# The routed experts of a Hyena block: results kept in SBUF, four chunks of 64 groups

## The reference

```python
grouped = x.reshape(B, g, t, d)                     # 256 groups of t = 32 tokens, d = 512
logits = jnp.einsum('bgtd,des->bgtes', grouped, controller) + tie
perm = (logits == jnp.max(logits, axis=-3, keepdims=True)).astype(x.dtype)
dispatched = jnp.einsum('bgtd,bgtes->bgesd', grouped, perm)
inner = jax.nn.relu(jnp.einsum('bgesd,desf->bgesf', dispatched, f1) + bias)
intermediate = jnp.einsum('bgesf,esfd->bgesd', inner, f2)
out = jnp.einsum('bgesd,bgtes->bgtd', intermediate, perm)
x = _layernorm(x + out)
```

## Time and profile before

| | |
|---|---|
| Runs | 2234.15, 2235.25, 2236.55 us; median 2235.25 us |
| Span of the profiled execution | 2229.5 us (its own time around the span isn't listed; the median of the runs is 5.75 us above it) |
| Mean granted clock of TensorE | 0.916 |
| Busy | PE 1895.0 us, DVE 1405.8, ACT 933.4, POOL 513.0 |
| Moved | 513.73 MB, mean 230 GB/s |

### The profile page before, as it was taken

How to read it: one execution, slowest core, us unless ns; L and a number is a source line. 1 busy time by engine, 2 the same in 40 slices (tenths; PEclk the granted TensorE clock), 3 DMA queues, 4 the chain that set the end, 5 groups by cost and what they waited for, 6 DMA issues and landing times. The chain is left out here.

```text
span 2229.5 us, 34871 instructions
## 1 busy us (share of the span) xinstructions
PE 1895.0 (85%) x12342; PEld 1285.3 (58%) x12342; DVE 1405.8 (63%) x2748; ACT 933.4 (42%) x1755; POOL 513.0 (23%) x410
## 2 busy tenths in 40 slices
PE   7999999999999699999969999996757676576444
PEld 6777777777777443444458888885636352352000
DVE  5877777877778454555558889885434354354344
ACT  4444444444444344444445555552323232242222
POOL 0100010001000044454455555551302020020000
PEclk9999999999999899999999999998889797697555
DMA  5134233333333577888767777773997999999999
GB/s 167 67 116 140 100 114 114 126 116 114 107 114 113 175 202 226 221 243 229 208 196 248 246 245 237 237 243 136 356 392 286 383 336 413 405 326 413 373 391 344
DMA packets 287298, 513.73 MB, mean 230 GB/s; under 512 B 26480, under 2 KB 105366, under 8 KB 278806
## 3 DMA queue, kind: packets, MB, share of 16 engines
q1 hardware_dynamic: 277909, 494.71, 65.8%
q10 hardware_dynamic: 9216, 16.78, 2.0%
HBM read 309.78 MB, written 201.62 MB: 229 GB/s over the span
## 5 line engine op out<-in xcount | busy, mean ns | idle before, releaser
L90 PE MATMUL p_pu<-p_xT_high,p_win_high 128*128 128x512 f32 (+1 forms) x816 | 329.9, 404 | 14.2 <-DVE p_win_low L85 12.0
L91 PE MATMUL p_pu<-p_xT_high,p_win_low 128*128 128x512 f32 (+1 forms) x816 | 313.3, 384 | 0.0
L92 PE MATMUL p_pu<-p_xT_low,p_win_high 128*128 128x512 f32 (+1 forms) x816 | 313.1, 384 | 0.0
L447 ACT ACTIVATE p_t<-p_pu,p_tbias,p_taps 128x512 f32<-128x512 f32 (+1 forms) x192 | 146.5, 763 | 358.2 <-PE p_pu L92 357.3
L85 POOL TENSOR_TENSOR p_xT_low<-p_xT,p_xT_high 128x2048 fp32r<-128x2048 f32 (+1 forms) x16 | 71.3, 4456 | 618.0 <-ACT p_xT_high L80 618.0
L564 DVE SCALAR_TENSOR_TENSOR p_t<-p_pu,p_taps,p_t 128x256 f32<-128x256 f32 (+1 forms) x384 | 208.6, 543 | 6.8
L849 POOL TENSOR_TENSOR q_y<-q_y 128x512 f32<-128x512 f32 x128 | 160.2, 1270 | 194.8 <-DVE q_y L870 194.8
L90 PEld LDWEIGHTS p_pu<-p_xT_high,p_win_high 128*128 128x128 f32 x816 | 155.4, 190 | 46.8 <-DVE p_xT_low L85 10.2
L92 PEld LDWEIGHTS p_pu<-p_xT_low,p_win_high 128*128 128x128 f32 x816 | 154.9, 190 | 32.8
L91 PEld LDWEIGHTS p_pu<-p_xT_high,p_win_low 128*128 128x128 f32 x816 | 155.4, 190 | 25.4
L870 DVE TENSOR_TENSOR q_y<-q_pg,q_v 128x512 f32<-128x512 f32 x256 | 158.0, 674 | 2.1 <-PE q_pg L779 1.8
(11 more groups left out here) (144 smaller groups left out, 3773.7 us busy)
## 6 DMA issues: line engine op xcount, KB each, us to landing
s_I<-e_out SPq DMA_DIRECT2D x64, 1024.0 KB, 8.5
q_av<-s_SV SPq DMA_DIRECT2D x64, 512.0 KB, 4.3
s_Z<-q_z SPq DMA_DIRECT2D x128, 256.0 KB, 3.2
o_zin<-s_Z SPq DMA_DIRECT2D x64, 512.0 KB, 3.9
k_shared<-s_I SPq DMA_DIRECT2D x32, 1024.0 KB, 11.9
e_taken<-s_I SPq DMA_DIRECT2D x32, 1024.0 KB, 11.5
e_out<-s_X SPq DMA_DIRECT2D x48, 512.0 KB, 8.6
s_X<-p_t SPq DMA_DIRECT2D x64, 256.0 KB, 2.3
```

What stands on the lines that cost most here:

```text
L90: pe.matmul(out, a[0], b[0], start=start, stop=False)
L91: pe.matmul(out, a[1], b[0], start=False, stop=False)
L92: return pe.matmul(out, a[0], b[1], start=False, stop=stop)
L447: nc.scalar.activation(t[r][m % 2][:, c], pu[(W + n) % 3][:, c], ACT.Identity, bias=tbias[:, w:w + 1], scale=taps[:, w, 2:3]).then_inc(t_o ...
```

## The change

The experts phase is written anew, and the choices' turning at the end of `output_phase` goes.

- *Chunks.* Four chunks of 64 groups (`GC`), each with all 128 experts. The rows tile `taken` has the layout (d block, pair of groups, expert, group of the pair); a pair of groups is interleaved element by element. It keeps its size, 32768 floats per partition.
- *Choices.* K stays resident. Per half chunk PE turns eight blocks of it (`choices`), ACT copies them to `picked`, and POOL spreads them (`pick`). TOOK and TAKE are gone.
- *Dispatch.* 8 matmuls of 256 moving columns per tile; 16 tiles per chunk. The token rows are read once.
- *Layers.* 32 quads per chunk. `layer1` has 64 moving columns, read from `rows` as 32 pairs of 8 bytes, 1 KB apart. `hidden` writes the pair of experts of each 64 rows side by side, with zeros (or what the bias makes of them, cancelled by `back`) where rows and columns don't belong together, as one scalar_tensor_tensor. `layer2` has the second weights as stationary operand (64 rows x 128 columns) and the hidden values as the moving one (128 columns), so the result comes out with d on the partitions, and one copy puts it over the quad's dispatched rows in `rows`. Scratch I is gone. The weights are loaded once per chunk, four times in all.
- *Turn.* Before the combine of a tile, PE turns its results back, 16 blocks of 128 x 128 per tile, reading every second element of `rows` as stationary operand; ACT and DVE copy them to one of three tiles `it`.
- *Combine.* As before, with K as stationary operand and `it` as moving. Turns and combines of a chunk are interleaved with the dispatch of the next, one tile of each per step; those of the last chunk stand alone.
- *PSUM.* Choices, dispatch, layer 2 and turns share a ring of three pairs of banks (`pun`); every unit has a number and a taker, ACT or DVE. Layer 1 and combine share two more banks, cleared by `clear` once per chunk.

```diff
-    pt = [ps(f"pt{s}", [P, 4, ES]) for s in range(2)] + pc
...
-            for v in range(2 * UNITS):
-                turn_take(v)
...
-            for u in range(UNITS):
-                store_unit(u)
...
+    GC = 64
+    CHUNKS = G // GC
+    TC = GC * GT // P
+    GP = GC // 2
+    NU, NF, NX, NI, NP, NR, NL, NX0 = 3, 4, 2, 3, 2, 3, 8, 8
...
+        rows = taken[:].rearrange("p (k b e g) -> p k b e g", k=DT, b=GP, e=ES)
...
+        def numbered():
+            for c in range(CHUNKS + 1):
+                if c < CHUNKS:
+                    yield "pick", c, 0, ON_ACT
+                for m in range(TC + 1):
+                    if c and m < TC:
+                        yield "turn", c - 1, 2 * m, ON_ACT
+                        yield "turn", c - 1, 2 * m + 1, ON_DVE if c < CHUNKS or m % 2 else ON_ACT
+                    if c < CHUNKS and m:
+                        yield "send", c, 2 * m - 2, ON_ACT
+                        if m == TC // 2 - 1:
+                            yield "pick", c, 1, ON_ACT
+                        yield "send", c, 2 * m - 1, ON_ACT if c and m % 2 else ON_DVE
+                if c < CHUNKS:
+                    for i in range(Q):
+                        yield "quad", c, i, (ON_ACT, ON_DVE)[i % 2]
...
             def load_weights(n):
-                s = n % NF
                 if n >= NF:
-                    sp.wait_ge(o_ps, ONE + n - NF + 1)
-                sp.dma_start(ff[s], A["ffn_f"][:, n % Q]).then_inc(ff_in[s], 16)
+                    b = n - NF
+                    sp.wait_ge(u_ps, ONE + number["quad", b // Q, b % Q] + 1)
+                sp.dma_start(ff[n % NF][:], A["ffn_f"][:, n % Q]).then_inc(ff_in[n % NF], 16)
...
+                if m >= LATE:
+                    x = (m - LATE) % NL
...
+                    if m >= NR:
+                        sp.wait_ge(res_st[m % NR], ONE + m // NR * 16)
+                    sp.dma_start(res_of(m), xr[m]).then_inc(res_in[m % NR], 16)
...
+            def bank_pair(u):
+                if u >= NU:
+                    pe.wait_ge(taken_ok[taker[u - NU]], ONE + taken_by[u - NU])
+                return pun[u % NU]
...
+            def choices(c, b):
...
+                    x = pe.transpose(to[:, m, :], K[:, t:t + P], ident[:])
...
+                        w = pe.matmul(to[:, h, a * 2 * ES:(a + 1) * 2 * ES], x[r, k * P:(k + 1) * P],
+                                      pick[j % NP][r].rearrange("p e g -> p (e g)"), start=True, stop=True)
...
-                        m = pe.matmul(ph[s][r, :], ff[w][:, 0, k * P + e * EF:k * P + (e + 1) * EF],
-                                      rows[:, k, 4 * i + e, :], start=(k == 0), stop=(k == DT - 1))
+                        x = pe.matmul(to[r, :, e % 2, :], ff[w][:, 0, k * P + e * EF:k * P + (e + 1) * EF],
+                                      rows[:, k, :, 4 * i + e, :], start=(k == 0), stop=(k == DT - 1))
...
-                    m = pe.matmul(po[e // 2][:, e % 2, :], hid[s][r, :], ff[w][r, 1, :],
-                                  start=True, stop=True)
+                        x = pe.matmul(to[:, h, k * P:(k + 1) * P], ff[w][r, 1, k * P:(k + 1) * P], hid[s][r, :],
+                                      start=True, stop=True)
...
+            def turn(c, n):
+                to = bank_pair(number["turn", c, n])
+                for g in range(2):
+                    for k in range(DT):
+                        x = pe.transpose(to[:, g, k * P:(k + 1) * P], rows[:, k, n, :, g], ident[:])
+                x.then_inc(u_ps, 1)
...
+                    x = pe.matmul(pq[j % 2][r, :], K[:, j * P + g * GT:j * P + (g + 1) * GT], it[n % NI][:, g % 2, :],
+                                  start=True, stop=True)
...
+                for m in range(TC + 1):
+                    if c and m < TC:
+                        turn(c - 1, 2 * m)
+                        turn(c - 1, 2 * m + 1)
+                    if c < CHUNKS and m:
+                        dispatch(c, 2 * m - 2)
+                        if m == TC // 2 - 1:
+                            choices(c, 1)
+                        dispatch(c, 2 * m - 1)
+                    if c and c < CHUNKS and m < TC:
+                        combine(c - 1, m)
+                    if c == CHUNKS and m:
+                        combine(c - 1, m - 1)
...
+                dve.scalar_tensor_tensor(hid[n % 2][:].rearrange("p (b x) -> p b x", x=4), ph[n % 2].rearrange("p (b x) -> p b x", x=4),
+                                         nbias[:, i:i + 1], back[:, i:i + 1, :].to_broadcast([P, GP, 4]), ALU.max, ALU.add
+                                         ).then_inc(hid_ok, 1)
```

More of the change, by code:

```diff
@@ L884, in output_phase @@
     UNITS = N1 // UG
[L885 removed]
+    NZ, NR = 3, 6
     with ExitStack() as ctx:
@@ L1122, in _ @@
                     finish(n - 1)
-            for u in range(UNITS):
-                keep_took(act, nc.scalar.copy, 2 * u)
         @block.vector
@@ L1517, in _ @@
[L1517 to L1534 removed]
+            pe.wait_ge(consts, ONE + 48)
@@ L1568, in _, with take @@
-            for m in range(NT0, NT):
-                close(m)
-            finish(NT - 1)
+                act.dma_start(dst[m], res_of(m)).then_inc(stored_to(m), 16)
+            def take(kind, c, n):
+                keep(act, nc.scalar.copy, ON_ACT, kind, c, n)
+            for c in range(CHUNKS + 1):
+                behind = 1 if c < CHUNKS else 2
+                if c < CHUNKS:
+                    take("pick", c, 0)
+                for m in range(TC + behind):
+                    j = (c - 1) * TC + m - behind
+                    if c and m < TC:
+                        take("turn", c - 1, 2 * m)
+                    if c and m >= behind:
+                        root(j)
+                    if c and m < TC:
+                        take("turn", c - 1, 2 * m + 1)
+                    if c < CHUNKS and m:
+                        take("send", c, 2 * m - 2)
+                        if m == TC // 2 - 1:
+                            take("pick", c, 1)
+                    if c and m >= behind:
+                        finish(j)
+                    if c < CHUNKS and m:
+                        take("send", c, 2 * m - 1)
+                if c < CHUNKS:
+                    for i in range(Q):
+                        take("quad", c, i)
@@ new lines, in take @@
+            def take(kind, c, n):
+                keep(dve, dve.tensor_copy, ON_DVE, kind, c, n)
+            clear(0)
+            dve.wait_ge(consts, ONE + 48)
+            step = Steps(dve, prep)
+            step(dve.tensor_scalar(nbias[:], bias[:], 0.0, None, ALU.min))
+            step(dve.tensor_scalar(bias[:], bias[:], 0.0, None, ALU.max))
+            for x in range(4):
+                step(dve.scalar_tensor_tensor(back[:, :, x], bias[:], side[:, x // 2:x // 2 + 1], nbias[:], ALU.mult, ALU.add))
@@ new lines, in _ @@
+            step(dve.tensor_tensor(bias[:], bias[:], nbias[:], ALU.add))
+            dve.tensor_scalar(nbias[:], bias[:], -1.0, None, ALU.mult).then_inc(back_ok, 1)
+            dve.wait_ge(back_ok, ONE + 1)
+            for c in range(CHUNKS + 1):
+                behind = 1 if c < CHUNKS else 2
+                for m in range(TC + behind):
+                    j = (c - 1) * TC + m - behind
+                    if c and m < TC:
+                        take("turn", c - 1, 2 * m + 1)
+                    if c and m >= behind:
+                        scale(j)
+                    if c < CHUNKS and m:
+                        take("send", c, 2 * m - 1)
+                    if c and behind - 1 <= m < TC + behind - 1:
+                        add(j + 1)
+                        if c < CHUNKS and m == TC - 1:
+                            clear(c)
+                        moments(j + 1)
+                if c == CHUNKS:
+                    break
```

535 lines of the change are left out of this document (200 added, 335 removed).

## The result

The changed kernel takes 2202.0 us (median of 4 runs, 2195.9 to 2208.5) against 2235.4 us of the kernel before on the same chip: a ratio of 0.985, 95% interval 0.982 to 0.987. In a second set on another chip the ratio was 0.986 (0.985 to 0.988). It is 1.5% faster, 33 us, where 51 us were predicted. The profiled execution took 2200.1 us, 1.8 us of it around the span.

A forecast was written before the change was run, and what follows sets the result against it. Transfers bound the experts phase before; afterwards engines would, stage by stage. Start 1550.5 + dispatch 31 + layers 268 + crossings 255 + last stage 64 = 2168.5, with joints 2179, with 5.75 around the span 2184 us; range 2125 to 2260.

The forecast's parts named there:

- I price each stage by its engines: Whole experts phase: DMA stops being the bound, with 112 MB in 297 us, so engine work sets each stage's time.
- A 512 KB load lands in 3.9 us where the queue is not full: Layer stages: landing time of one weight load, taken from the DFT's rows of the profile before.
- pitch >= 2.05: Layer stages: each load has two pitches to land, 3.9 us plus 0.2 handshake; 2.05 us a quad, 268 us in all.
- the sum of 1.90: Layer stages: PE's work per quad, layer 1 0.64, layer 2 0.91 and tiling changes 0.35 us.
- The interlock (0.2): Crossing stages: three engines stand near 4.8 us a step, so 0.2 us is added for mutual waiting, giving 5.0.
- The form changes (0.3): Crossing stages: two further changes of PE's tiling form per step, 0.3 us within PE's sum of 4.8.
- Rival 3: Crossing and last stages: three engines interlock, steps 5.9 and 4.4 us, +56, 2240 us; chance 0.16 of 5.5 or more.
- I take nothing: Turns in crossing stages: reading every second element costs nothing extra, out of a possible 0 to 1.72 us a step.
- rival 1: Turns: strided reads double their time, 1.72 us over 64 steps, 110 us more, 2294 us; chance 0.12.
- rival 4: Last stage: clock stays at 1.2 GHz, PE 5.7 us a step, +34, 2218 us; chance 0.06.
- The 10 us for joints: Whole phase: 11 joints between stages and the first cold matmuls, 10 us added to the span.
- Rival 5: Layers and crossings: layer 1 at streaming rate, loads in 3.4 us, pitch 1.80, steps 4.8; 2142 us; chance 0.20.

The follow-up runs named there:

- three tiles: The changed kernel with three weight tiles (NF = 3) instead of four; 2277.7 us, measured once.
- the deeper ring: The changed kernel with seven weight tiles instead of four, the three idle `it` tiles taking weights during the layers; 2156.8 us, 0.967 of before.

## Why the prediction was right, and where it was not

- **The total.** The direction and the range were right; of the 51 us that were forecast 33 came. That the total is off by no more than 18 us is in part luck: the start and the stages up to the last crossing took 35 us more than forecast, and the last stage and two margins 19 us less.
- **What bounds.** Right. Transfers stopped being the bound, at 180 GB/s over the phase. But "I price each stage by its engines" was true of three kinds of stage and not of the layers, where the latency of a load decides. There PE is busy for 0.83 to 0.84 where over 0.85 was the sign.
- **Layers.** The stages took 26 us more than forecast, more than the whole miss. Two steps failed. The first is "A 512 KB load lands in 3.9 us where the queue is not full", and with it "pitch >= 2.05". It lands in 4.5, and the pitch is 2.20 where nothing else is in the way: the mechanism was the right one, a term mis-sized. The second is that the loads for the next stage, issued in the middle of a layer stage, have no term: they cost 3.6 us in each, 14 us of the 26 (read from the traces: the long pitch is at the same quad of every stage, and one quad earlier with three tiles; no run left these loads out). The formula was wrong too: with 3.9 the right one gives (3.9 + 1.82 + 0.2) / 3 = 1.97. For PE the sum of 1.90 was close to the 1.82. Its 0.85 us of layer 2's work, from which the form changes of 0.35 come, stands in no row. Layer 1 is bound by its columns (0.43 us for 32 of them, 0.72 for 64), of which a constant 0.14 is a part; 0.64 was the middle of two bounds and near it by luck. The Trainium skill (TensorE: Matmul & The Clock Gate, Part 1) has a floor of 25 ns between matmul starts, 0.80 us for 32; the measured 0.43 us for 32 records, 13 ns each, in four column groups, does not agree.
- **Crossing stages.** 5.0 a step against 5.04: right, with two errors that cancel. The interlock (0.2) doesn't exist: the norm's 1.8 us of other engines taken away left the step at 5.04. The turns' stride, put at nothing, costs 0.22. The form changes (0.3) are there, inside the times from start to start: the turns were taken at 1.72 us and cost 2.11, of which 0.22 are the stride, and 1.89 are left when contiguous; the dispatch costs 1.93, where 32 records of the first chunk start within 3.45 us, 1.73 a tile. Rival 3 falls.
- **The turns' stride.** "I take nothing" was wrong by 69 ns a load (209 against 140), some 0.22 us a step and 12 us in all. Its ground, the dispatch's strided writes to PSUM, was another path, and the analogy did not carry. The sign for rival 1 was wrong as well: a mean load of 215 ns was to mean a doubling, 110 us; 209 came, and a tenth of the price. From one turn's record to the next the distance grew only from 109 to 120 ns. The note on cachelines (SBUF — State Buffer, in the Trainium skill) has two hits on a 16-byte line for full rate. The trace doesn't agree for stationary reads, two hits at a stride of two floats. For moving reads without a second hit, 512 bytes apart, it agrees in kind: 2.10 us against 0.72.
- **Last stage.** 3.6 us a step from ScalarE was wrong; it is 3.16 in the mean, TensorE's 3.11 and a little for ScalarE, whose own bound is some 3.1. The clock did not fall to half: 0.94 over the stage, so rival 4 falls, and with waits for transfers gone the sum of 59.1 lies under the 64.
- **Start, dispatch, margins.** Within 2 us each. For the start that is luck: its terms add up to 1548.2 and not to 1550.5, and they measured 10.2 us for 6.2 (5.6 from the first issue to the first turn of choices, of which 2.5 are the bias load's place in the queue). The 10 us for joints were already in the stages, and the 5.75 us around the span compared a median with one execution: the executions here have 1.8, one 2.2.
- **Rival 5** had a pitch of 1.80, close to TensorE's clean 1.82, with layer 1 bound by its columns as it is, but needed loads in 3.4 us; the deeper ring reached its side without them, and then TensorE's stops took part of it.

## What to carry to other kernels

A ring of NF buffers that is refilled when a step ends has a pitch of (landing + the step's own work) / (NF - 1), or that of the work if it is longer: when a change makes the steps shorter, count the buffers again, and look for tiles that are idle in that stage. Here that was worth 45 us, more than the change itself. Look also at what else is issued into the same queue in that stage: five small loads a stage cost 14 us here, and a mean over the stage hid them. A transfer kept in SBUF is paid for in the layout: ask of every new read how far apart its elements lie, the moving operand's above all. And where the bound moves from DMA to TensorE, the saving is not the transfers' cost but what is left of it after the engine's new work, here 33 of 200 us.

## What the runs showed of the hardware

- A moving operand of single floats 512 bytes apart ran at about a third of the rate of pairs 1 KB apart (2.10 us against 0.72 for 32 records of 64 columns).
- A stationary operand with a stride of two floats loads in 209 ns where a contiguous one takes 140; 16 such turns took 0.22 us more.
- At 266 to 272 GB/s of weights TensorE stopped for up to 2.2 us at a time, 11.5 us in a run, and 29.7 us when it did more instructions per us; with the transfers cut to 38 to 45 GB/s stops of 0.3 to 0.6 us were left. Each ended 1.2 to 1.6 us after a 16 KB packet of the instruction queue had landed. An engine that does many small instructions beside heavy transfers can be stopped in a way that no semaphore shows.
